# First expert layer: 384 rows of an expert as three pieces of 128 partitions instead of four of 96, and slots for its work counted anew

## What is computed

```python
xg = x.reshape(bsz, H, n, d).transpose(1, 0, 2, 3).reshape(H, S, d)   # H = 4 groups of S = 1024 tokens
combine, dispatch = top2_dispatch(xf, Wg, C)                          # C = 86 places per expert and group
h = relu(layer_norm(moe_apply(xf, combine, dispatch, W1, b1), lw, lb))   # 24 experts, 128 -> 512
out = moe_apply(h, combine, dispatch, W2, b2)                            # 24 experts, 512 -> 128
```

## Time and profile before

| | us |
|---|---|
| median of 3 runs | 1465.71 |
| lowest, highest | 1464.28, 1469.84 |
| span of the profiled execution | 1465.0 |
| busy in that span: TensorE, VectorE, ScalarE, GpSimd | 1277.5, 1227.2, 856.9, 661.9 |

### The profile page before, as it was taken

The page is one execution under the profiler, slowest core; times in us unless marked ns, Lnnn a source line. Parts: engine busy times, 40 slices in busy tenths (PEclk is TensorE's granted clock), DMA queues, the critical chain, the costliest instruction groups (busy, mean ns, idle before and its releaser), DMA issues. The chain is left out here.

```text
span 1465.0 us, 21638 instructions
## 1 busy us (share of the span) xinstructions
PE 1277.5 (87%) x7304; PEld 888.3 (61%) x7304; DVE 1227.2 (84%) x2515; ACT 856.9 (58%) x2077; POOL 661.9 (45%) x612
## 2 busy tenths in 40 slices
PE   6977888897887976899897895599999999999997
PEld 5533444453433444788887774467676777777776
DVE  6678999998999899999997778869988555568877
ACT  5357757665798885556654658554464444444462
POOL 0018555605489855664751775339600322147300
PEclk9997999999999877999999898699999999999999
DMA  6003545545244422454552520300020233113201
GB/s 230 1 21 87 147 128 147 141 122 153 82 126 126 123 87 68 126 155 135 146 146 72 190 53 13 119 7 1 2 59 1 60 89 107 41 38 49 25 16 43
DMA packets 75747, 127.50 MB, mean 87 GB/s; under 512 B 11486, under 2 KB 38334, under 8 KB 75030
## 3 DMA queue, kind: packets, MB, share of 16 engines
q1 hardware_dynamic: 56182, 75.24, 17.0%
q0 software_dynamic: 19456, 50.88, 13.2%
HBM read 85.71 MB, written 40.37 MB: 86 GB/s over the span
## 5 line engine op out<-in xcount | busy, mean ns | idle before, releaser
L672 DVE TENSOR_TENSOR_SCAN sc_st<-sc_dA,sc_st 128x1024 f32<-128x1024 f32 x128 | 287.3, 2284 | 0.0
L2164 DVE COPY at_pT<-at_p_t 128x512 f32<-128x512 f32 (+1 forms) x192 | 109.0, 598 | 107.8 <-PE at_p_t L2046 107.4
L1270 POOL DMA_INDIRECT g_state<-xn_scratch,moe_tab x96 | 119.6, 1246 | 174.3 <-POOLq L99 102.4
L2059 PEld LDWEIGHTS at_p_o<-at_V,at_pT 128*128 128x128 f32 x1280 | 154.4, 194 | 31.1 <-issue 30.8
L444 ACT ACTIVATE sc_dA<-sc_dt,g_state 128x511 f32<-128x511 f32 x256 | 168.9, 710 | 7.2 <-DVE sc_st L672 5.3
L650 DVE TENSOR_TENSOR sc_st<-sc_st,sc_p_bc 128x1024 f32<-128x1024 f32 x128 | 154.9, 1211 | 13.4 <-PE sc_p_bc L501 13.2
L640 DVE TENSOR_TENSOR sc_st<-sc_u,sc_p_bc 128x1024 f32<-128x1024 f32 x128 | 154.3, 1206 | 6.6 <-PE sc_p_y L532 6.3
L1310 POOL DMA_INDIRECT g_state<-r_scratch,moe_tab x96 | 121.5, 1266 | 83.6 <-PE e_bank L1409 56.7
L2059 PE MATMUL at_p_o<-at_V,at_pT 128*128 128x128 f32 x1280 | 155.0, 277 | 3.6 <-DVE g_state L2153 3.6
L2026 PE MATMUL at_p_s<-att_xaT,at_qT 128*128 128x512 f32 (+3 forms) x512 | 150.7, 437 | 0.0
L501 PE MATMUL sc_p_bc<-sc_bc,mamba_sel 96*128 96x512 bf16 x256 | 104.9, 411 | 50.5 <-DVE sc_st L640 48.6
(11 more groups left out here) (304 smaller groups left out, 2615.0 us busy)
## 6 DMA issues: line engine op xcount, KB each, us to landing
y_scratch<-g_state SPq DMA_DIRECT2D x24, 768.0 KB, 5.2
g_state<-W SPq DMA_DIRECT2D x48, 256.0 KB, 5.5
r_scratch<-g_state SPq DMA_DIRECT2D x16, 512.0 KB, 3.6
y_scratch<-g_state SPq DMA_DIRECT2D x24, 192.0 KB, 2.8
xn_scratch<-g_state SPq DMA_DIRECT2D x16, 256.0 KB, 4.9
g_state<-x SPq DMA_DIRECT2D x4, 512.0 KB, 7.5
g_state<-xn_scratch SPq DMA_DIRECT2D x8, 256.0 KB, 5.2
g_state<-x SPq DMA_DIRECT2D x1, 2048.0 KB, 12.7
```

The costliest lines, as they stand in the source:

```text
L672: nc.vector.tensor_tensor_scan(st[:, m % RS, :, :].rearrange("p a b -> p (a b)"), dA[:, m % 4, :, :].rearrange("p a b -> p (a b)"), st[:, ...
L1270: nc.gpsimd.indirect_dma_start(out=self.xg[:, e % 4, h, :], out_offset=None, in_=self.xn_rows, in_offset=bass.IndirectOffsetOnAxis(ap=r.ta ...
L2059: ins = nc.tensor.matmul(p_o[:, i, :], pT[:, n % 2, bank, c + (i - j) * P:c + (i - j + 1) * P], V[:, b % 2, j, h * D:(h + 1) * D], start=( ...
L2164: v.tensor_copy(pT[:, n % 2, part, 0:cols], p_t[:, PT_BANK[part], 0:cols]).then_inc(pT_ready, 1)
```

## The change

An expert's 4 x 96 rows are numbered through, 0 to 383, and cut into `CK = 3` pieces of 128 rows. Group h's 96 places lie at rows 96 h, so in the routing table they fall into one or two pieces: `PLACES` cuts groups 1 to 3 into a part of 32 places and one of 64 each. The table then takes 7 matmuls for each of 16 (tile, choice) pairs where it took 4. Gathers, transposes, matmuls, evacuations and the second layer's work go by pieces of 128, 72 in each layer. The results lie in memory by expert and row.

The slots are counted anew: every engine of the experts has the same number of slots in a step, 4 in odd steps and in steps 26 to 41, else 3. The first layer takes slots 0 to 71, the units start at slot 76, the second layer takes slots 160 to 231. ScalarE works off one piece a slot.

The core of the diff (renamed loop bounds, shapes and semaphore counts that follow from 4 -> 3 and 96 -> 128 are left out):

```diff
+ROWS0 = HG * CP
+CK = ROWS0 // P
+
+PLACES = [[(0, CP, 0, 0)], [(0, 32, 0, 96), (32, CP, 1, 0)], [(0, 64, 1, 64), (64, CP, 2, 0)],
+          [(0, 32, 2, 32), (32, CP, 2, 64)]]
...
-PE_SLOTS, ACT_SLOTS, DVE_SLOTS = 4, 2, 2
-EVEN_FROM, EVEN_TO, FIRST_WINDOW = 22, 43, 26
-def uneven(i):
-    return not EVEN_FROM <= i < EVEN_TO
+UNIT_SLOTS = 4
+WIDE_FROM, WIDE_TO = 26, 42
+def slots(i):
+    return 4 if i % 2 or WIDE_FROM <= i < WIDE_TO else 3
+STEP_OF = [i for i in range(B * DS // 2) for _ in range(slots(i))]
...
@@ scan_stage, scalar_steps
                 yield
+                yield
                 if i + 1 < STEPS:
                     decays(i + 1, 1)
-                yield
-                if i % 4 == 3 and uneven(i) or i == EVEN_FROM - 2:
-                    yield
+                yield from [None] * (slots(i) - 2)
...
@@ scan_stage, tensor_steps
                 if i + 1 < STEPS:
                     broadcast_b(i + 1, 1)
-                yield
-                yield
-                if i % 2 and uneven(i):
-                    yield
-                if i == EVEN_FROM - 2:
-                    yield
-                    yield
+                yield from [None] * (slots(i) - 2)
...
@@ Routing0.tensor
                 for k in range(2):
-                    ins = nc.tensor.matmul(p_t[:, h * 2 * E0:(h + 1) * 2 * E0], self.A[k][:, t, :],
-                                           self.R[k][:, t, :, :].rearrange("p a b -> p (a b)"),
-                                           start=(i == 0 and k == 0), stop=(i == steps - 1 and k == 1))
+                    for first, end, piece, row in PLACES[h]:
+                        ins = nc.tensor.matmul(p_t[row:row + end - first, piece * 2 * E0:(piece + 1) * 2 * E0],
+                                               self.A[k][:, t, first:end],
+                                               self.R[k][:, t, :, :].rearrange("p a b -> p (a b)"),
+                                               start=(i == 0 and k == 0), stop=(i == steps - 1 and k == 1))
...
@@ Moe0Experts.weigh
-            wait_window(FIRST_WINDOW + u)
+            wait_window(STEP_OF[(CK * E0 + UNIT_SLOTS) + UNIT_SLOTS * (u + 4)])
...
@@ Moe0Experts.tensor
-                nc.tensor.matmul(bank[0:CP, k % 2, :], self.xgT[:, e % 2, h * CP:(h + 1) * CP],
+                nc.tensor.matmul(bank[:, k % 2, :], self.xgT[:, e % 2, h * P:(h + 1) * P],
                                  self.w1[:, e % 3, :], start=True, stop=True).then_inc(self.piece_made, 1)
-                if h == 3 and e + 1 < E0:
+                if h == CK - 1 and e + 1 < E0:
                     turn(e + 1)
                 yield
...
@@ Moe0Experts.scalar
                     self.piece_read, 1)
-                if h == 1:
-                    yield
-            if e + 1 < E0:
-                copy_turned(e + 1)
-            yield
+                if h == CK - 1 and e + 1 < E0:
+                    copy_turned(e + 1)
+                yield
...
@@ Moe0Experts.vector
-        yield from [None] * (DVE_SLOTS * (E0 + 1))
+        yield from [None] * (CK * E0 + UNIT_SLOTS)
...
-            yield
-            yield
+            yield from [None] * UNIT_SLOTS
...
@@ program
-        y1_dram = dram("y1_scratch", [HG, E0, CP, HID])
+        y1_dram = dram("y1_scratch", [E0, ROWS0, HID])
```

More of the change, by code:

```diff
@@ L1267, in gather_x @@
             if e >= 4:
-                pool.wait_ge(self.piece_made, 5 * (e - 4) + 1)
-            for h in range(HG):
+                pool.wait_ge(self.piece_made, (CK + 1) * (e - 4) + 1)
+            for h in range(CK):
                 nc.gpsimd.indirect_dma_start(
@@ L1307, in gather_r @@
             if e >= 3:
-                pool.wait_ge(self.turned2, HG * (e - 2))
-            for h in range(HG):
+                pool.wait_ge(self.turned2, CK * (e - 2))
+            for h in range(CK):
                 nc.gpsimd.indirect_dma_start(
@@ L1342, in turn @@
         def turn(e):
-            k = 5 * e
+            k = (CK + 1) * e
             if e:
                 pe.wait_ge(self.piece_read, k - 1)
-            pe.wait_ge(self.gathered1[e % 4], 16 * HG * (e // 4 + 1))
-            for g in range(HG):
-                ins = nc.tensor.transpose(bank[:, k % 2, g * CP:(g + 1) * CP], self.xg[:, e % 4, g, :],
-                                          w["ident"][0:CP, 0:CP])
+            pe.wait_ge(self.gathered1[e % 4], 16 * CK * (e // 4 + 1))
+            for g in range(CK):
+                ins = nc.tensor.transpose(bank[:, k % 2, g * P:(g + 1) * P], self.xg[:, e % 4, g, :], w["ident"])
             ins.then_inc(self.piece_made, 1)
@@ L1384, in tensor @@
                 yield
-        yield from [None] * PE_SLOTS
+        yield from [None] * UNIT_SLOTS
         def product(n):
-            e, h = divmod(n, HG)
+            e, h = divmod(n, CK)
             pe.wait_ge(self.rT_ready, n + 1)
@@ L1395, in product @@
             for f in range(FC):
-                ins = nc.tensor.matmul(bank[0:CP, 1, h * D:(h + 1) * D], self.rT[:, n % 3, f * CP:(f + 1) * CP],
+                ins = nc.tensor.matmul(bank[:, 1, h * D:(h + 1) * D], self.rT[:, n % 3, f * P:(f + 1) * P],
                                        self.w2[:, e % 3, f, :], start=(f == 0), stop=(f == FC - 1))
             ins.then_inc(self.product2, 1)
-        for n in range(E0 * HG):
-            e, h = divmod(n, HG)
+        for n in range(E0 * CK):
+            e, h = divmod(n, CK)
             if h == 0:
-                pe.wait_ge(self.gathered2[e % 3], 16 * HG * (e // 3 + 1))
+                pe.wait_ge(self.gathered2[e % 3], 16 * CK * (e // 3 + 1))
             if n:
@@ L1414, in tensor @@
             yield
-        product(E0 * HG - 1)
+        product(E0 * CK - 1)
     def scalar(self, act):
@@ L1489, in scalar @@
         act.wait_ge(self.eps_set, 1)
-        yield from [None] * ACT_SLOTS
+        yield from [None] * UNIT_SLOTS
         for u in range(self.UNITS + 4):
@@ L1523, in scalar @@
             yield
-        yield from [None] * ACT_SLOTS
+            yield
+        yield from [None] * UNIT_SLOTS
         def copy_out(e):
-            act.wait_ge(self.product2, HG * (e + 1))
+            act.wait_ge(self.product2, CK * (e + 1))
             if e >= 2:
                 act.wait_ge(self.stored2[e % 2], 16 * (e // 2))
-            nc.scalar.activation(self.out2[:, e % 2, :, :].rearrange("p a b -> p (a b)"), bank[0:CP, 1, :],
+            nc.scalar.activation(self.out2[:, e % 2, :, :].rearrange("p a b -> p (a b)"), bank[:, 1, 0:CK * D],
                                  ACT.Copy).then_inc(self.out2_ready, 1)
         for e in range(E0):
-            for h in range(HG):
-                n = HG * e + h
+            for h in range(CK):
+                n = CK * e + h
                 act.wait_ge(self.turned2, n + 1)
@@ L2745, in laid_out @@
         "pcol": np.arange(P, dtype=np.float32)[:, None].copy(),
[L2746 removed]
+        "group_base": np.tile(np.arange(HG, dtype=np.float32) * CP, (P, 1)),
         "sel": c(sel.reshape(96, 2 * DS * P)),
```

73 lines of the change are left out of this document (36 added, 37 removed).

## The result

The changed kernel takes 1495.39 us (1493.19 to 1497.86) beside 1466.28 of the kernel before: 1.0196 times as long, with an interval of 1.0177 to 1.0215. The forecast was 1461 with a range up to 1472, so it missed the time and the sign. The profiled spans are 1491.4 and 1465.0 us, 26.4 apart.

The account below looks back on a forecast made before the run. VectorE's own work was taken to bound the scan stage, its 19.5 us of waits the most to gain there; -2 -5.9 -7 +10.3 = -4.6 us gave 1461 us against the median, range 1450 to 1472.

Parts of the forecast that it names:

- The two expert layers: Scan steps 0 to 20 and 42 to 63: fewer expert pieces remove some of VectorE's 5.0 us of waits, -2 us.
- Step 21: Change of layers: the last expert piece ends 5.1 us earlier, so VectorE's stall before tile 0 goes, -5.9 us.
- The table: Front stage's table of rows: alternating 32- and 64-column matmuls wait at each width change, 13.2 us long, +10.3 us.
- the bound only, the low clock: Front stage's table: if TensorE's clock falls meanwhile, it takes 25 us, +22 us; an upper end, not the term taken.
- Rival B: Front stage's table: narrow matmuls don't wait for each other, table costs +1 us, total 1452 us; chance 0.22.
- The rest of the middle: Steps 21 to 41 beyond the change of layers: tiles half a step later end waits and idle time, -7 of 8.6 us.
- D: Rival for the middle: no gain, as ScalarE waits for the later tiles and hands the delay on, 1468 us; chance 0.20.
- my own sign that the prediction falls: Stated test: the prediction falls if the table is short or the middle's second tile is late for ScalarE.
- C: Rival for the expert layers: an idler TensorE's clock falls behind each softplus step, 14.2 us lost, 1477 us; chance 0.08.

Follow-up runs that it names:

- before_cut: Kernel before the change, only its table's groups 1 to 3 cut into alternating 64- and 32-column matmuls: 1482.65 us, 1.0115.
- as_before: Changed kernel with the middle's units placed as in the kernel before, experts and table as changed: 1475.86 us, 1.0065.
- own_steps_late: Changed kernel; in the middle alone TensorE's once-a-batch scan steps (dt_project, turn_y, x_project) moved behind the second sum of states: 1475.62 us, 1.0067.
- own_table: Changed kernel with the middle's once-a-batch TensorE scan steps behind the second sum and the table's pieces sorted by width: 1462.71 us, 0.9973.
- own_all_table: Changed kernel with once-a-batch TensorE scan steps behind the second sum in all pair steps, table pieces sorted by width: 1463.61 us, 0.9975.
- tiles_later: Changed kernel with TensorE's middle tiles one slot later, both behind the second sum from unit 4 on: 1480.41 us, 1.0101.
- scalar_own_first: Changed kernel; in the middle ScalarE does the scan's own steps before emptying the two tiles, nothing moved on TensorE: 1477.98 us, 1.0083.
- kept_busy: Changed kernel plus 14 extra identity products on TensorE in six middle pair steps, ahead of steps that wait for ScalarE: 1481.64 us, 1.0090.
- table_order: Changed kernel with the table's same 112 matmuls sorted by width, so the width changes 2 times: 1478.06 us, 1.0093.
- later_table: Changed kernel with TensorE's middle tiles one slot later and the table's pieces sorted by width: 1468.67 us, 1.0022.

## Why the prediction was wrong

**The two expert layers** (-2): -0.9 and -1.0. The size fits, and so does the cover: VectorE is busy 206.75 of 209.5 us. But so little can't be told from one profile each: the second layer of `before_cut`, whose code there is that of the kernel before, also took 0.9 us less.

**Step 21** (-5.9): right, mechanism and size. The last piece ends 6.7 us earlier (5.1 forecast), the gathered rows are there, tile 0 starts 6.6 us earlier, the wait is gone. `as_before` and `own_steps_late` keep this gain; in the profiles of `own_table` and `own_all_table` 3.5 and 1.9 us of it are lost again, and why stays open.

**The table** (+10.3): the mechanism was right, the term too small, 13.9. The distance between two starts was right: 0.13 us estimated, 126 and 140 ns measured at full clock. What I took for the bound only, the low clock, came true in part: from about 73 us on the distances are 153 and 179 ns, which makes the stretch 15.69 us and not some 13.3 (an estimate, all of it at the full-clock distances), and the products behind the table run at half clock until about 89, so that VectorE waited 3.94 us for its first convolution and not 1.42. Here the rule of the Trainium skill that I had set beside the row (TensorEngine Tiling (Array Packing), Key Properties: changing the tiling mode, not just the tile, drains TensorE) agrees with both runs: 64 to 32 columns in turn 126 to 140 ns, the same widths in a row 32 and 25. Rival B fell with it.

**The rest of the middle** (-7): this is the step that failed; it became some +21 (29.9 us of waits for 8.6). I worked it out on one step, 32, and there it came out: step 32 of the changed kernel has no wait of VectorE over 0.1 us, and those of the bias matmul for ScalarE are gone. Two things were missing.

First, I counted the sum of states only as 1.04 us between two tiles, a delay of the second tile for ScalarE. I didn't ask who waits for the sum once a tile stands ahead of it. It is VectorE, and its only cover is its two scans (4.45 us) with what statistics and softplus add. `tiles_later` shows this half: with the tile behind the sum, 29.9 us of waits for sums become 3.8.

Second, the middle has steps of another kind. In two thirds of them TensorE's queue has a step of the scan near its start that needs ScalarE. With the tiles in the last gap and the next first gap, TensorE came to it late enough. With both tiles done early and ScalarE later, it idles 2.8 to 4.2 us in seven; six of the seven cost VectorE a wait. `own_steps_late` and `scalar_own_first` show this half: without the idle time 7.5 and 8.9 us are left. So the idle time ahead of low clock, which I said would go, came in a new place.

The rivals had the pieces, apart. D had ScalarE wait for the later tiles and hand the delay on (53.6 us for 8.6, so my own sign that the prediction falls came, the second tile late for ScalarE), but let it cost no more than the gain. C had low clock make the sum late for VectorE, but in the two expert layers, where it stayed small: the five waits there sum to 3.5 us. Neither joined the two: delay of ScalarE, idle TensorE, low clock and late start, tile ahead of the sum, VectorE. The Trainium skill (TensorE: Matmul & The Clock Gate, Part 1: the throttled clock is what idling returns to) agrees with the link between idle and clock in step 27, where the granted clock is 0.88 in the window from 416 to 418, in which TensorE does nothing, and 0.50 in the next. That a low clock can also come in a stretch whose records are busy throughout, as in the table, I had allowed for as a bound, without a row for it.

What stays open: step 23. Its tile stands ahead of the sum behind an `x_project` that ran at low clock, after 5.47 us in which TensorE waited for VectorE, which had a softplus to do. It lost 5.4 us in the changed kernel, 5.3 in `kept_busy` and `scalar_own_first`, 2.6 in `table_order`, and 2.0 in `own_steps_late`, where this `x_project` too stands behind the sum. `tiles_later` and `as_before`, which move the tiles, have no wait there. I have not tried it by itself.

## What to carry to other kernels

When work is moved past another instruction of the same queue, price it by who waits for that other instruction, at low clock as well as at full, and in every kind of step that the stretch has, not only in the one whose rows are at hand. When matrices are cut anew, put the pieces of one width together: some 95 changes between 64 and 32 columns cost the front stage 14 us here, with the low clock that came with them, and with 2 changes its first scan starts as early as before. And if a change brings two losses, mend each by itself before judging the whole: the three pieces of 128 are worth 0.25 to 0.45% in the four best of the runs that put both right, and lose 0.2% in the fifth (`later_table`).

## What the runs showed of the hardware

Changes between weights of 64 and 32 columns cost some 105 ns each, and a row of them brought TensorE's granted clock down to 0.50 with no idle time in its records at all (5.00 of 5.00 us busy from 74 to 79 us); the same 112 matmuls sorted by width left it at 1.00. Back to back, a bf16 matmul of 48 moving columns starts 45 ns after the one before with 96 columns of weights, 32 with 64 and 25 with 32: the spacing changed with the weights while the 48 columns stayed. And the clock doesn't always fall within the idle time. Before step 27 of the changed kernel it did (0.88 from 416 to 418 us, all idle); in `kept_busy` the same step had 1.05 us of idle time up to 417.45, the clock was 1.00 to 418, 0.92 from 418 to 420 and 0.50 after that, with TensorE at work in between. That this idle time was what brought it down is not shown.
